# An attention and mixture kernel whose opening is rebuilt: the gate's first layer turned round, tiles normalised on GpSimd, statistics in two parts, the first attention chains woven in

## What is computed

```
x = L0_attn_x                                            # (32, 256, 128)
mod = (_silu(L0_c) @ L0_wmod).reshape(32, 6, 1, -1)      # sa, ca, ga, sb, cb, gb; the same for layer 1
ga = (2 * (ga >= 0) - 1) * jnp.maximum(jnp.abs(ga), 0.25)
h = _layernorm(x, axis=-1) * (1 + ca) + sa
Q, K, V = proj(Wq, bq), proj(Wk, bk), proj(Wv, bv)       # of h, 16 heads of 8
Qn = Q / jnp.maximum(jnp.linalg.norm(Q, axis=-1, keepdims=True), EPS)     # Kn alike
attn = jax.nn.softmax(jnp.einsum('bhqd,bhkd->bhqk', Qn, Kn) / jnp.sqrt(jnp.float32(dk)), axis=-1)
head_outs = jnp.einsum('bhqk,bhkd->bhqd', attn, V)
hidden = jax.nn.gelu(h @ Wg1.T + bg1, approximate=False)                  # (32, 256, 64)
gate_dynamic = jax.nn.sigmoid((hidden @ Wg2.T + bg2).mean(axis=1))        # a mean over all tokens of a batch
head_outs = head_outs * (jax.nn.sigmoid(g) * gate_dynamic)
x = x + ga * (out @ Wo.T + bo)
```

## Time and profile before

| | us |
|---|---|
| three executions | 1863.12, 1866.05, 1871.23 |
| median | 1866.05 |
| profiled execution, its own time | 1869.96 |
| its span from first to last instruction | 1867.6 |
| before the gate stage | 0 to 50 |
| gate stage | 50 to 112 |
| chains of the first three batches | 112 to 134 |
| attention loop of layer 0 | from 134 |

### The profile page before, as it was taken

The page is one execution under the profiler, slowest core; times in us unless marked ns, Lnnn a source line. Parts: engine busy times, 40 slices in busy tenths (PEclk is TensorE's granted clock), DMA queues, the critical chain, the costliest instruction groups (busy, mean ns, idle before and its releaser), DMA issues.

```text
span 1867.6 us, 38682 instructions
## 1 busy us (share of the span) xinstructions
PE 1590.4 (85%) x12775; PEld 812.6 (44%) x12775; DVE 1286.5 (69%) x3330; ACT 1159.9 (62%) x1846; POOL 889.6 (48%) x1699
## 2 busy tenths in 40 slices
PE   1979999999994999968999999999999724999970
PEld 1843444444432344423444444444444312766750
DVE  6546677777755788864676677776677653777758
ACT  1437778788773889953556566565555353787850
POOL 2344444545431233333444435847548553666654
PEclk9999999999997999978999999999899856999995
DMA  6012112112111990012221222322223222322328
GB/s 198 1 21 49 35 35 41 41 35 44 38 35 46 373 386 31 1 45 49 49 46 41 41 46 48 74 46 58 47 50 71 73 79 97 91 91 86 91 72 259
DMA packets 234370, 142.96 MB, mean 77 GB/s; under 512 B 183939, under 2 KB 201347, under 8 KB 233157
## 3 DMA queue, kind: packets, MB, share of 16 engines
q1 hardware_dynamic: 222464, 120.67, 24.8%
q0 software_dynamic: 9088, 18.89, 3.2%
q10 hardware_dynamic: 2628, 1.00, 0.2%
HBM read 38.64 MB, written 59.90 MB: 53 GB/s over the span
## 4 chain that ended last, share of the span: by engine, by line
PE 46%; DVE 10%; issue 4%; POOL 3%; DVEq 1%; ACT 1%; DMA 1%; POOLq 1%; SPq 0%; ACTq 0%
PE OP L2142 8%; PE OP L2316 6%; PE SP L2301 5%; DVE mx L1319 5%; PE OP L2007 5%; PE SP L1987 4%; PE M L2105 4%; PE M L2080 2%; PE SP L2122 2%; PE M L2096 2%; PE M L2101 2%; POOL h_dram L483 2%; PE OP L2154 1%; PE M L1997 1%; PE M L2291 1%
## 5 line engine op out<-in xcount | busy, mean ns | idle before, releaser
L856 ACT ACTIVATE pt<-SP 128x768 f32<-128x768 f32 x256 | 207.4, 810 | 252.5 <-PE SP L2122 252.4
L1319 DVE TENSOR_REDUCE mx<-M 128x2 f32<-128x512 f32 (+1 forms) x384 | 257.8, 682 | 107.3 <-PE M L2105 104.2
L522 POOL TENSOR_SCALAR_AFFINE_SELECT pt<-pt 128x256 f32<-128x256 f32 x512 | 198.9, 413 | 266.6 <-ACT pt L856 264.8
L748 ACT ACTIVATE pt<-SP 128x1024 f32<-128x1024 f32 x256 | 256.2, 1020 | 78.0 <-PE SP L1887 78.0
L553 POOL DMA_INDIRECT y_dram<-hT,dest x156 | 150.2, 963 | 113.6 <-DVE hT L1612 77.1
L1906 PE MATMUL OP<-pt,vs 128*32 128x256 f32 x1408 | 185.2, 385 | 0.0
L954 ACT ACTIVATE pt<-SP,b 128x512 f16<-128x512 f32 x156 | 107.3, 688 | 87.8 <-PE SP L2301 61.5
L483 POOL DMA_INDIRECT h_dram<-hT,slot x128 | 129.8, 1014 | 57.8 <-issue 31.7
L2142 PE MATMUL OP<-pt,vs 128*32 128x128 f32 (+1 forms) x1408 | 149.8, 335 | 4.9 <-POOL pt L522 4.9
L1606 DVE TENSOR_TENSOR pt<-vs,pt 128x512 f16<-128x512 f32 x156 | 107.8, 691 | 56.2 <-ACT vs L955 56.1
L643 POOL TENSOR_TENSOR st<-st,ksT 128x512 f32<-128x512 f32 x48 | 72.0, 1500 | 153.1 <-DVE ksT L1737 153.0
(11 more groups left out here) (324 smaller groups left out, 3381.5 us busy)
## 6 DMA issues: line engine op xcount, KB each, us to landing
h_dram<-shared SPq DMA_DIRECT2D x8, 4488.0 KB, 33.7
hT<-h_dram SPq DMA_DIRECT2D x39, 264.0 KB
rows<-g_dram SPq DMA_DIRECT2D x4, 2048.0 KB, 7.3
pt<-y_dram SPq DMA_DIRECT2D x32, 256.0 KB, 3.6
x_sb<-in_x SPq DMA_DIRECT2D x8, 512.0 KB, 8.8
pt<-in_w SPq DMA_DIRECT2D x4, 1024.0 KB, 5.7
out<-x_sb SPq DMA_DIRECT2D x16, 256.0 KB, 3.0
y_dram<-hT,dest POOLq DMA_INDIRECT x156
```

Source lines behind the costliest of these rows:

```text
L522: last = pool.affine_select(out=diag, in_=diag, compare_op=ALU.is_ge, fill=0.0, base=0, pattern=[[0, 2], [1, P]], channel_multiplier=-1)
L748: act.activation(pt[:, u % 4], SP[u % 2][:], ACT.Exp, scale=SCALE).then_inc(s["exp"], 1)
L856: act.activation(pt[:, u % 4, :, 0:384], SP[u % 2][:, :, 0:384], ACT.Exp, scale=SCALE).then_inc(s["exp"], 1)
L1319: dve.tensor_reduce(to, M[:, k % 2, :].rearrange("p (j k) -> p j k", j=4 if k < 4 else 2), AX.X, ALU.max).then_inc(s["mred"], 1)
```

## The change

- **Gate stage.** `hcur` and `keep` go: ACT writes straight to `hT`. The gate's first layer is turned round: its weights are stationary and 256 tokens move, so the output has 64 partitions, ACT adds the bias and sums over tokens in the gelu instruction itself (`accum_out=gsum`), and the bias addition, the product with ones and its copy go. The product comes two steps behind the turn. The loops are written out.
- **Normalising** moves from VectorE to GpSimd (`ln`), and waits for statistics in two parts: tiles 0 to 23 (batches 0 to 11) and 24 to 63.
- **First chains.** The projections of batches 0, 1, 2 stand behind steps 4, 11, 20 of PE's gate stage; `square` and `high` behind steps 9, 17, 20, 26 of ACT's; GpSimd does the lengths of batch 0 behind the 14th normalisation and those of 1 and 2 behind the last; VectorE has `take`, `lengths`, `unit`, `low` between its statistics.
- **VectorE's order.** The conditions come first, no longer behind the wait for `LOADS`; gains and bias rows come late, between the first chains.
- **Experts' weights.** Two parts are staged at other places of `shared`, two in `ksT`. Rounding moves into the attention loop: ACT behind the last exponential of batches 0 to 3, GpSimd behind the lengths in its turns 1 to 4.
- **PE** runs twelve products of 512 bf16 columns, whose result nobody reads, between the gate's last product and the first scores.

SP's program keeps its order.

```diff
-            def weight_low(l):
...
+            def weight_low(c):
...
-            weight_low(0)
...
+                def ln(b):
+
+                    n = norm_s[0]
+                    pool.wait_ge(n["stat"], 1 if b < 12 else 2)
+                    if b >= 2:
+                        pool.wait_ge(n["zT"], b - 1)
+                    for t in range(TT):
+                        k = slice(TT * b + t, TT * b + t + 1)
+                        last = pool.tensor_scalar(z[:, b % 2, t, :], x_sb[:, TT * b + t, :], mean[:, k], rstd[:, k],
+                                                  ALU.subtract, ALU.mult)
+                    last.then_inc(n["z"], 1)
+
+                for b in range(B):
+                    ln(b)
+                    if b == 13:
+                        lengths(0)
+                        place_v(0)
+                lengths(1)
+                place_v(1)
                 lengths(2)
                 for b in range(B):
...
+                    if 1 <= b <= CHUNKS:
+                        weight_low(b - 1)
...
-            for c in range(CHUNKS):
-                weight_high(0, c)
+                act.wait_ge(s["zT"], b + 1)
+                act.activation(hT[:, b * T:(b + 1) * T], bank[b % 2][:, 0:T], ACT.Identity,
+                               bias=modT[0][:, SA, b:b + 1], scale=modT[0][:, CA, b:b + 1]).then_inc(s["h"], 1)
...
+                act.wait_ge(s["x"], b + 1)
+                act.activation(gact[:, b % 2], bank[2 + b % 2][0:HID, 0:T], ACT.Gelu, bias=bx[0][:, 0:1],
+                               accum_out=gsum[:, b:b + 1]).then_inc(s["gelu"], 1)
...
+                steps = {9: [(square, 0)], 17: [(square, 1)], 20: [(high, 0)], 26: [(square, 2)]}
...
+                    if b < CHUNKS:
+                        weight_high(0, b)
...
+            conditions()
+            blanks()
+            first_stats(range(3))
             dve.drain()
...
+            statistics(slice(0, 24))
+            dve.drain().then_inc(norm_s[0]["stat"], 1)
+            modulations()
...
+                first_stats(range(3, 6))
                 take(0)
+                first_stats(range(6, 8))
                 lengths(0)
+                dve.drain()
+                statistics(slice(24, NT))
+                dve.drain().then_inc(norm_s[0]["stat"], 1)
                 take(1)
                 lengths(1)
                 unit(0)
                 low(0)
+                gains()
                 dve.drain()
                 take(2)
                 lengths(2)
+                bias_rows()
+                static_gate()
                 unit(1)
                 low(1)
...
+                pe.matmul(bank[2 + b % 2][0:HID, 0:T], wx[0][:], hT[:, b * T:(b + 1) * T],
+                          start=True, stop=True).then_inc(s["x"], 1)
...
+                for n in range(B + 2):
+                    gates(n)
+                    if n in (4, 11, 20):
+                        for t in range(TT):
+                            project((4, 11, 20).index(n), t)
...
+                for _ in range(12):
+                    pe.matmul(OP[:, 1, :].rearrange("p (n q) -> p n q", n=4), identb[:],
+                              maskQ[:].unsqueeze(1).to_broadcast([P, 4, P]), start=True, stop=True, skip_group_check=True)
```

More of the change, by code:

```diff
@@ L558, in spread_y @@
                     pool.tensor_tensor(yb[:, c % 4, 0], yb[:, c % 4, 0], yb[:, c % 4, 1], ALU.add).then_inc(k["sum"], 1)
-            def keep():
-                s = norm_s[0]
-                def one(b, par):
-                    pool.wait_ge(s["h"], b + 1)
-                    pool.tensor_tensor(hT[:, bass.ts(b, T)], hcur[:, par, :], one_s[:, 0:T],
-                                       ALU.mult).then_inc(s["hT"], 1)
-                with pool.Fori(0, B // 4) as i:
-                    for k in range(4):
-                        one(4 * i + k, k % 2)
             def dense():
@@ L617, in low @@
                     pool.tensor_tensor(h16[:, 1, n], hcur[:, n % 2, :], h16[:, 0, n], ALU.subtract).then_inc(s["low"], 1)
-                for b in range(2):
-                    lengths(b)
-                    place_v(b)
+                def ln(b):
[15 more added lines that the diff above has]
+                place_v(1)
                 lengths(2)
@@ L649, in experts @@
                     one(g, g % 2)
-            keep()
             dense()
@@ L678, in weight_high, with norm @@
                 act.activation(stage(l, c), stage(l, c), ACT.Copy, scale=WSCALE).then_inc(s["whi"], 1)
[L680 removed]
+            def norm(b):
                 s = norm_s[0]
[L684 to L708 removed]
@@ L770, in enter @@
                     last.then_inc(s["h"], 1)
-                square(0)
-                square(1)
-                high(0)
-                square(2)
+                steps = {9: [(square, 0)], 17: [(square, 1)], 20: [(high, 0)], 26: [(square, 2)]}
+                for n in range(B + 2):
+                    gates(n)
+                    for step, b in steps.get(n, []):
+                        step(b)
+                sigmoid()
                 high(1)
@@ new lines, in static_gate @@
+            def static_gate():
+                dve.wait_ge(gl_mm, 1)
+                dve.scalar_tensor_tensor(gl[:], bank[4][0:B, 0:H], 1.0 / T, bg2[:], ALU.mult, ALU.add).then_inc(gl_in, 1)
+                dve.wait_ge(gl_exp, 1)
+                dve.tensor_scalar(gl[:], gl[:], 1.0, None, ALU.add)
+                dve.drain()
+                dve.scalar_tensor_tensor(gs[:], gs[:], 1.0, gl[:], ALU.add, ALU.mult)
+                dve.drain()
+                dve.reciprocal(gs[:], gs[:]).then_inc(gl_fin, 1)
@@ L1856, in _, with gate @@
-            norm()
-            pe.wait_ge(norm_s[0]["gsum"], B)
-            pe.matmul(bank[6][0:B, 0:H], gsum[:], wg2[:], start=True, stop=True).then_inc(gl_mm, 1)
+                pe.wait_ge(s["z"], b + 1)
+                if b >= 2:
+                    pe.wait_ge(s["h"], b - 1)
+                for t in range(TT):
+                    last = pe.transpose(bank[b % 2][:, t * P:(t + 1) * P], z[:, b % 2, t, :], ident[:])
+                last.then_inc(s["zT"], 1)
+            def gate(b):
+                s = norm_s[0]
+                pe.wait_ge(s["h"], b + 1)
+                if b >= 2:
+                    pe.wait_ge(s["gelu"], b - 1)
+                pe.matmul(bank[2 + b % 2][0:HID, 0:T], wx[0][:], hT[:, b * T:(b + 1) * T],
+                          start=True, stop=True).then_inc(s["x"], 1)
@@ L1860, in dense, with gates @@
+            def gates(n):
+                if n < B:
+                    norm(n)
+                if n >= 2:
+                    gate(n - 2)
             def dense():
```

257 lines of the change are left out of this document (83 added, 174 removed).

## The result

The changed kernel takes 1848.2 us (median of 14 runs, 1840.1 to 1869.7); beside it the kernel before took 1870.1 (14 runs). The ratio is 0.9884, 95% interval 0.9864 to 0.9904: 21.8 us less, where the prediction's sum said 32.5. So it is faster, just inside the range of 1819 to 1849 and outside the forecast's own 1827 to 1842, and a third of the forecast gain is missing. In the profiled execution 7.0 us of it are missing by the first scores, 5.8 more go in the attention loop, 1.1 behind it; 0.6 come back outside the span.

A forecast was written before the change was run, and what follows sets the result against it. PE was taken to bound the gate stage, and a chain of small steps what follows. Gate stage 25.0 plus woven chain 9.9, less 2.4 in the loop, gave 32.5 us: 1834 from 1866.05, own range 1827 to 1842.

The forecast's parts named there:

- the second rival: Gate stage: GpSimd bounds from 0.62 per normalisation; at 0.9 turn 1.95, 1847 us; chance 0.17, shared with a late chain.
- PE's turn: Gate stage, per batch: transposes 0.48 plus two passes of 256 columns 0.91, so 1.39 us, 32 turns 44.5.
- stall of the second statistics: Gate stage: PE reaches batch 12 at 45.7, its normalised z is ready at 48.2; stall 2.5 us.
- stall of the lengths: Gate stage: GpSimd's lengths behind batch 13 keep it until 55.5, PE is out at 51.0; stall 4.5 us.
- The opening: Start of gate stage: x's third part lands at 14.9, statistics of 24 tiles at 21.3, first transpose at 24.5.
- The normalisation: Gate stage, GpSimd: 0.35 us per 128 columns, two per batch 0.7, hidden behind PE's turn.
- The clock: Gate stage: lower clock assumed; rival that it rises to 2.4 GHz, 12 us less, 1822 us, chance 0.20.
- The woven chain: Gate to scores: batch 0's chain done by about 67, so the 9.9 us wait goes; a late chain gives 1844.
- From gl_fin to the scores: Behind the gate stage: 10.6 us stay, because the gate's DMAs stand ahead in SP's queue; scores at 99.1.
- The loop: Attention loop: GpSimd's weight rounding costs 1.2 us each in batches 3 and 5, 2.4 together; ACT's rounding is hidden.
- is entered at the lower clock and stays there: Attention loop, rival "slower": some 11 us more per batch, four batches over 0.5% slower than now; chance 0.04.
- the mark set beforehand: Sign: scores at 99 but time falling by less than 28 means the loop or later stages took it back.

The follow-up runs named there:

- five edits: Changed kernel plus batch 0's lengths behind normalisations, second statistics first, transposing DMAs before the gate's way, weights' rounding before the loop, product-and-sum normalisation: 1812.8 us, ratio 0.9687.
- With constants: Changed kernel with GpSimd's normalisation taking constants 0 and 1 instead of each row's mean and reciprocal deviation; ran once, no ratio, last gelu at 84.8.
- unwoven kernel: Changed kernel with the first three batches' chains put back behind the gate stage and second statistics directly behind the first: 1837.9 us, ratio 0.9835.

## Why the prediction was right in direction and short by a third

That the time lies inside the range is in part luck. 1848.2 is beyond the forecast's own 1827 to 1842 and next to the 1847 of the second rival, and the kernel before, 1866.05 in the three executions that the prediction started from, is 1870.1 over 14.

The same forecast steps, with what was measured (profiled execution; gains of 32.5 and 19.2):

| step | forecast | measured |
|---|---|---|
| statistics of 24 tiles, first transpose | 21.3, 24.5 | 22.6, 25.8 |
| PE's turn | 1.39, PE the bound | 1.55, GpSimd the bound |
| GpSimd's normalisation | 0.35 | 0.78 (0.85 with the stretched ones) |
| a projection in the stage | 2.74 | 1.56, all three |
| stall of the second statistics | 2.5 | 4.57 |
| stall of the lengths | 4.5 | 5.61 |
| last gelu ends | 86.0 | 92.9 |
| gl_fin, from there to the scores | 88.5, 10.6 | 95.5, 10.6 |
| first scores | 99.1 | 106.05 |
| gained by then | 34.9 | 27.9 |
| lost in the loop | 2.4 | 8.2 |

- *The opening* was right but for 1.3 us: x's third part was ready at 16.92 by VectorE's wait, 2 later than the 14.9 of the earlier trace rows.
- *The normalisation* was mis-sized, by a factor 2.2, and this is the step that cost most: with the form that costs 0.44 the stage is 14.2 us shorter. The stretching of GpSimd's operations beside VectorE, which the prediction had only in the width of its range, took 3.7 more. The fault was to take a row as near because it "reads one tensor", without looking at its two operations. The rival, "from 0.62 GpSimd is the bound; at 0.9 the turn is 1.95", was true by its condition, not by its turn, since the clock rose too. Of the Trainium skill (GPSIMD Engine Reference, 4.1 Engine selection) neither half fits: against VectorE's 0.30 the form used costs a factor 2.6, product and sum 1.5.
- *The clock* rose, at 32, which I gave 0.20. It took 1.18 off each projection and some off PE's turn under GpSimd's, so it could not bring the 12 us of that rival. The rule of the Trainium skill (TensorE: Matmul & The Clock Gate, Part 1), that the clock goes up once PE is kept busy, agrees with 32.80 here and still not with the 60 busy us of before. The two rivals were each half true and offset one another, so the sum hit the stage closer than its terms deserved.
- *The stalls* were both there, from 45.1 to 49.64 and from 53.0 to 58.65 where 45.7 to 48.2 and 51.0 to 55.5 were worked out, with the releasers said. Together they are 3.2 longer than said.
- *The woven chain.* The prediction split its gain in 25.0 for the stage and 9.9 for weaving. But it had charged 8.2 for projections and 4.5 for the lengths to the stage: by its own numbers weaving cost 12.7 and brought 9.9. The split hid that a part of the change works against it. Measured: 10.1 against 7.9.
- *From gl_fin to the scores*: 10.6, as said, and for the reason said.
- *The loop.* The delay was there, and smaller than said: PE's waits in batches 3 and 5 grew by 0.95 and 0.87 (1.90 to 2.85, 0.78 to 1.65), where 1.2 each was said, and of the 0.95 only 0.62 goes when the rounding goes. What failed is the price of a wait. I took 1 us of waiting as 1 us; behind it the clock fell, and batches 3 to 5 lost 6.1. The fall was a rival only as a loop that "is entered at the lower clock and stays there". The kernel before enters it so too, and against it that start cost PE 0.6. ScalarE's rounding, said to be hidden, put batch 1's first exponential off by about the 0.8 that are left in batch 0.
- *Behind the loop* another 1.1 us went (19.7 at batch 31, 18.6 in the span). I did not follow it.

By the mark set beforehand ("scores at 99 and less than 28") the scores were late already; the loop then took back its part.

## What to carry to other kernels

Before work is moved to an engine, find a row with the same two operations and operands, not one of the same size; and price each part of a change against the part it displaces, so that one that costs 10.1 and brings 7.9 is seen. Where PE is busy without gaps, ask of every wait that grows whether the clock survives it. Judge several edits by marks in the trace and not by adding up medians. The medians say 35 us for five edits that alone gave 1 to 9 each, some 21 together, which looks like more than the sum. But each of these has an uncertainty of 5 to 10 us. Counted from the first transpose to batch 31 the five gained 34.1 together and 9.2, 6.1, 4.8, 7.5 and 13.8 alone, 41.4: less than the sum. Only in the gate stage was it a little more.

## What the runs showed of the hardware

- GpSimd, 128x128 fp32, two scalars per partition: subtraction and product 0.79 us, product and sum 0.44. With constants subtraction and product still take 0.64. Two tensors of 256 columns: 0.61.
- The same 0.79 became 1.18 to 1.53 in seven of 64 cases, each time beside VectorE's operations on SBUF. In the unwoven kernel VectorE makes the gains and bias rows sooner, and there it is the four normalisations from 37.0 to 43.1 that take 0.95 to 2.15. That the two engines disturb each other is read from this coincidence; no run took VectorE's work away.
- A gelu that also sums its row is followed by an own instruction that reads the sum, 0.19 us. It is overlapped: ScalarE's three instructions of a turn, 1.22 us together, repeat after 0.95 in the kernel with five edits (41.52 to 42.47).
- TensorE's clock rose to the higher level at 32 us in the stage whose product is two passes of 256 columns a batch, and never in 60 us of the stage with four of 64 columns, though PE was busier there. Why is open: no run separated width from the rest.
- In batch 3 of the loop it fell in or right behind single waits of 2.49 to 2.94 us in ten kernels of ten, behind 2.23 in one of three, not behind 1.90. In batch 5 it fell behind 1.74 to 1.76 in seven of seven, not behind 1.65 or less, and in the changed kernel's stage at 76.5 and 86.8, with 1.45 and 1.66 as the longest waits there. So the length of one wait alone doesn't say whether it falls.
- Four transposing DMAs took SP 5.23 us to issue at 99.56, and 7.66 at 80.96, right behind the DMA of the gains' rows (issued at 80.57).
